# Two adapter products in one accumulation: all high-part products of a unit ahead of all low-part products

## The reference

```
w   = L0_cond_weight[itok]               # one 1024 x 1024 matrix for each of 8 samples
y   = einsum('bsi,boi->bso', x, w)       # x: 8 x 256 x 1024
t   = y.reshape(2048, 1024)[:, perm].reshape(2048, 16, 64)
t   = gelu(einsum('bhd,hdm->bhm', t, up))     # up: 16 x 64 x 256
t   = einsum('bhm,hmd->bhd', t, down)         # down: 16 x 256 x 64
out = x + t.reshape(2048, 1024)[:, unperm]
```

## Time and profile before

| | before |
|---|---|
| median of three runs | 297.74 us (297.6 to 298.1) |
| span of the profiled execution | 296.1 us |
| median of the runs less that span | 1.6 us |
| TensorE matmul busy (PE) | 290.6 us, 98% |
| TensorE weight load busy (PEld) | 215.0 us, 73% |
| VectorE (DVE) | 179.2 us, 61% |
| ScalarE (ACT) | 159.9 us, 54% |
| GpSimd (POOL) | 98.8 us, 33% |

### The profile page before, as it was taken

The page is one execution under the profiler, slowest core; times in us unless marked ns, Lnnn a source line. Parts: engine busy times, 40 slices in busy tenths (PEclk is TensorE's granted clock), DMA queues, the critical chain, the costliest instruction groups (busy, mean ns, idle before and its releaser), DMA issues.

```text
span 296.1 us, 4358 instructions
## 1 busy us (share of the span) xinstructions
PE 290.6 (98%) x1694; PEld 215.0 (73%) x1694; DVE 179.2 (61%) x211; ACT 159.9 (54%) x179; POOL 98.8 (33%) x92
## 2 busy tenths in 40 slices
PE   8999999999999999999999999999999999999994
PEld 7788888888888838886488855888468885444441
DVE  3599679589778455973658726685446523343333
ACT  5655453466764368344584265822853207777750
POOL 4000000068552007860527007702473405222234
PEclk9999999999999999999999999999999999999999
DMA  7999999999988947799576973876752864421335
GB/s 206 363 402 421 395 421 422 366 320 375 394 328 277 378 153 197 281 360 406 212 249 196 345 311 114 312 237 199 244 191 83 286 185 122 128 71 71 144 142 212
DMA packets 23699, 77.87 MB, mean 263 GB/s; under 512 B 2688, under 2 KB 11264, under 8 KB 18816
## 3 DMA queue, kind: packets, MB, share of 16 engines
q1 hardware_dynamic: 7056, 43.39, 39.3%
q0 software_dynamic: 7488, 25.18, 24.7%
q10 hardware_dynamic: 9136, 9.05, 8.8%
HBM read 60.82 MB, written 16.78 MB: 262 GB/s over the span
## 4 chain that ended last, share of the span: by engine, by line
PE 95%; DMA 2%; SPq 1%; POOL 1%; issue 0%; DVE 0%; ACT 0%; POOLq 0%; DVEq 0%
PE ps L641 38%; PE ps L645 19%; PE ps L698 19%; PE ps L674 6%; PE ps L677 5%; PE ps L680 5%; PE ps L606 2%; DMA w_raw<-w 2%; PE ps L611 1%; POOL out_late L319 1%; SPq L223 1%; SPq L251 0%; DVE w_raw L528 0%; ACT w_hi L429 0%; POOLq L361 0%
## 5 line engine op out<-in xcount | busy, mean ns | idle before, releaser
L641 PE MATMUL ps<-x_pair,w_hi 128*128 128x512 f32 x480 | 131.5, 395 | 0.0
L381 ACT ACTIVATE w_hi<-w_raw 128x1024 fp32r<-128x1024 f32 x58 | 58.3, 1056 | 62.8 <-PE ps L645 51.6
L415 ACT ACTIVATE hidden<-ps 128x1024 f32<-128x1024 f32 x64 | 61.6, 1028 | 55.1 <-PE ps L680 47.1
L641 PEld LDWEIGHTS ps<-x_pair,w_hi 128*128 128x128 f32 x480 | 82.0, 189 | 12.8 <-issue 1.8
L645 PEld LDWEIGHTS ps<-x_pair,w_lo 128*128 128x128 f32 x480 | 73.6, 189 | 10.2
L490 DVE TENSOR_TENSOR w_lo<-w_raw,w_hi 128x1024 fp32r<-128x1024 f32 x60 | 71.0, 1222 | 11.8 <-ACT w_hi L381 10.7
L645 PE MATMUL ps<-x_pair,w_lo 128*128 128x256 f32 x480 | 76.3, 281 | 0.0
L292 POOL DMA_INDIRECT t_raw<-y_rows,idx x32 | 34.9, 1090 | 115.1 <-DMA y_rows<-y_out 82.4
L518 DVE TENSOR_REDUCE y_out<-ps 128x256 f32<-128x512 f32 x64 | 42.8, 685 | 24.5 <-PE ps L645 23.0
L698 PE MATMUL ps<-hidden,down_sb 128*64 128x512 f32 (+1 forms) x264 | 57.4, 583 | 0.0
L510 DVE TENSOR_TENSOR t_lo<-t_raw,t_hi 128x512 fp32r<-128x512 f32 x32 | 21.7, 694 | 47.9 <-ACT t_hi L405 42.5
(11 more groups left out here) (29 smaller groups left out, 119.4 us busy)
## 6 DMA issues: line engine op xcount, KB each, us to landing
w_raw<-w SPq DMA_DIRECT2D x29, 1024.0 KB
y_rows<-y_out ACTq DMA_DIRECT2D x32, 256.0 KB
x_raw<-x_cols SPq DMA_DIRECT2D x7, 1024.0 KB
w_raw<-w SPq DMA_DIRECT2D x4, 256.0 KB, 5.0
w_raw<-w SPq DMA_DIRECT2D x2, 512.0 KB, 7.7
hidden<-up SPq DMA_DIRECT2D x1, 1024.0 KB, 12.3
down_sb<-down SPq DMA_DIRECT2D x1, 1024.0 KB, 12.3
w_raw<-w SPq DMA_DIRECT2D x2, 384.0 KB, 6.9
```

The source lines that it names most:

```text
L381: nc.scalar.activation(w_hi[:, g % WS, k, :], w_raw[:, g % WRAW, k, :], ACT.Copy).then_inc(w_hi_done, 1)
L415: nc.scalar.activation(hidden[:, f % HS, m, :, :], up_banks(f, m)[:, :, :], ACT.Gelu).then_inc(gelu_done, 1)
L641: nc.tensor.matmul(acc, w_hi[:, ws, k, col], x_pair[:, xs, k, :, :], start=(k == 0), stop=False)
```

## The change

In `lora_unit`, all sixteen products with w_hi (both output tiles, eight blocks each) now come first, and all sixteen with w_lo after them. The number and the shapes of the products, their operands, and what each waits for are the same; what is changed is which product carries each wait, and when each output tile is finished. `lora_done` for o = 0 is now raised by the eighth low product of the unit, and for o = 1 by the last product, as before.

```diff
                 for o in range(OT):
                     col = slice(o * P, (o + 1) * P)
-                    acc = y_bank(g, o)
-                    for n in range(2):
-                        ks = range(n * HALF, (n + 1) * HALF)
-
-                        if o == 0:
-                            pe.wait_ge(w_hi_done, 2 * (g - PAIR) + n + 1)
-                        for k in ks:
-                            nc.tensor.matmul(acc, w_hi[:, ws, k, col], x_pair[:, xs, k, :, :], start=(k == 0), stop=False)
-                        if o == 0:
-                            pe.wait_ge(w_lo_done, 2 * (g - PAIR) + n + 1)
-                        for k in ks:
-                            last = nc.tensor.matmul(acc[:, 0, :], w_lo[:, ws, k, col], x_hi[:, xs, k, :], start=False, stop=(k == KT - 1))
+                    for k in range(KT):
+                        if o == 0 and k % HALF == 0:
+                            pe.wait_ge(w_hi_done, 2 * (g - PAIR) + k // HALF + 1)
+                        nc.tensor.matmul(y_bank(g, o), w_hi[:, ws, k, col], x_pair[:, xs, k, :, :], start=(k == 0), stop=False)
+                for o in range(OT):
+                    col = slice(o * P, (o + 1) * P)
+                    for k in range(KT):
+                        if o == 0 and k % HALF == 0:
+                            pe.wait_ge(w_lo_done, 2 * (g - PAIR) + k // HALF + 1)
+                        last = nc.tensor.matmul(y_bank(g, o)[:, 0, :], w_lo[:, ws, k, col], x_hi[:, xs, k, :], start=False, stop=(k == KT - 1))
                     last.then_inc(lora_done, 1)
```

## The result

| | before | after |
|---|---|---|
| median of seven runs each | 297.9 us (297.56 to 298.95) | 296.4 us (295.85 to 297.15) |
| ratio, 95% interval | | 0.9947 [0.9933, 0.9962] |
| span of the profiled execution | 296.1 us | 295.2 us |
| TensorE matmul busy | 290.6 us | 289.7 us |

The change makes the kernel 0.5% faster, 1.5 us between the medians. I had forecast 297.5 with a range from 296.6 to 299.1 and "no measurable change": wrong, on the fast side. Rival B, the cost of a switch that is paid less often, is the one that came in kind.

The account below looks back on a forecast made before the run. TensorE's row of products was taken as the bound, with no wait to remove. Runs of sixteen gave -0.3 us, all else 0, on a 296.1 us span plus 1.6 around it: 297.4, given as 297.5, range 296.6 to 299.1.

Parts of the forecast that it names:

- Rival B: Switches between high and low products cost 0.01 us and three of four go: -0.9 us, 296.8 us; chance 0.17.
- part 4: TensorE's reads of w_lo: first half wanted 3.7 us into the unit, not 0.93; no wait removed, gain 0.
- part 3: TensorE's reads of w_hi: second half wanted 0.93 us into the unit, not 1.40; still in time, cost 0.
- Part 5: Output tile 0 finished 4.65 us into the unit, not 2.8; VectorE's second sum stays where it is, cost 0.
- part 2: Runs of sixteen for runs of four: high run 3.69 us, low 1.91, unit 5.60 against 5.61; -0.3 us over thirty.
- The lower end: Low bound for runs of sixteen, fitted from 4 + 4 and 6 + 6 lengths: unit 5.585 us, -0.9 us in all.
- A: Within each unit's sixteen high and sixteen low products, long runs go slower: up to +1.8 us, 299.5 us; chance 0.14.
- C: In all units, long runs reach `down_unit`'s 0.219 us per high product: -10.5 us, 287.2 us; chance 0.03.
- E: A TensorE wait on w_lo is removed after all: a few tenths of a us at most, counted inside the forecast.

Follow-up runs that it names:

- e8: Changed kernel with odd units reordered: two high products (k = 0), all 16 low, then the other 14 high; 296.57 us, ratio 0.9958 to the kernel before.

## Why the prediction was wrong

**Right.** That TensorE's spacings are the whole matter and no wait is removed (part 4; the moved-back waits confirm it). That w_hi, wanted earlier, is in time (part 3). Part 5, by which VectorE's first sum stands about 4.87 us behind a unit's start: in unit 15, which starts at 94.50, the sums stand at

```profile
99.37 0.69 DVE L518 TENSOR_REDUCE y_out<-ps 128x256 f32<-128x512 f32 x1 [1.16 <-PE ps L643]
100.26 0.69 DVE L518 TENSOR_REDUCE y_out<-ps 128x256 f32<-128x512 f32 x1 [0.20 <-PE ps L643]
```

that is 4.87 us behind the start. Ahead of the second 0.20 are idle, where part 5 left 0.28; the second sum stayed at the end of its unit. The low run, forecast at 1.91 us, took 30.08 - 28.17 = 1.91.

**The step that failed** is the value taken in part 2, the high run of 3.69 us; it took 3.65. I carried on the pace of the third to sixth high product of the run of six, 0.230, as if it were settled. It was the tail of a transient: 0.2325 in the mean of the first four, and 0.2267 in the mean from the fifth on. The error is 0.04 us a unit, about 1.1 us in all, the whole difference between the 297.5 forecast and the 296.4 measured. The unit of 5.567 us is below 5.59, which the prediction had named as a sign of being wrong.

**The lower end was too near as well.** The fit 4p + c and 6p + c gave c = 9 ns and -0.9 us. It takes the cost of a return as the same in both runs. With the settled p of 0.3467 the 4 + 4 group has 1.403 - 1.387 = 0.016 and the 6 + 6 piece 2.10 - 2.08 = 0.02: the longer run had paid the whole transient, the shorter one not yet. A fit over two lengths of which neither is settled put part of the transient into the slope. That I set the better fit aside for its thin digits, and then took a number from rows just as thin, made it worse.

**The rivals.** A (long runs at 0.235) is refuted: the 0.235 is the start of a transient, and wide products hold 0.2267. B was right in kind, a cost at the switch; its size was 1.2 us over the thirty units, not 0.9. C did not come: the settled 0.2267 and 0.120 stay above the 0.219 and 0.1095 that C would have brought. They are also about 11 ns each above the estimates of 216 and 109 ns that the prediction worked out from the Trainium skill ("TensorE: Matmul & The Clock Gate", "Wait — 56ns, not 53.3ns?"). E is refuted.

**What the runs make of it.** Excess over the settled unit of 5.547 us:

| run length | returns to high in a unit | unit, us | excess, ns |
|---|---|---|---|
| 1 | 16 | 5.653 | 106 |
| 2 | 8 | 5.576 | 29 |
| 4 (before) | 4 | 5.613 | 66 |
| 8 | 2 | 5.587 | 40 |
| 16 (changed) | 1 | 5.567 | 20 |
| 2 and 30 high, 16 low (e8) | 1 (every second one for two products only) | 5.555 | 8 |
| any, one width | 0 | | 0 |

From four on, with low products of 256 columns, each return to the wide products costs 16 to 20 ns, and the gain follows from the number of returns: this is shown. For runs of two and one that rule fails, and why two is cheap is open. The spacings of the trace say only where. In nanoseconds, a unit of the changed kernel has high products of 233, 236, 228, 233 and 231, then eleven of 227, and low ones of 113 and 119, then fourteen of 120. The loss builds up over the first four or five wide products, and the first narrow ones behind them give part of it back, so a return cut off after two wide products hardly pays. What in the array or its queue makes that transient no run here tells.

## What to carry to other kernels

Where TensorE's products are what bounds a kernel, order products by their width: put those of one width in a row, and count the returns from narrow to wide. Here that held for runs of four and more; runs of two did nearly as well, so measure the orders. Before carrying a pace from a short run to a longer one, look whether it is still falling along the run, and if it is, give the range the room for it. Where the effect is a few ns per product, read it from the spacing over many units in the trace, since the start-up of this kernel alone scatters by more than the gain.

## What was not expected of the hardware

- A product of 128 x 512 fp32r values settles at 0.2267 us start to start, but takes 0.2325 in the mean for the first four behind narrower products. Behind an `up_unit` stage it is slow for longer: unit 12 of the changed kernel is 0.13 us above unit 13 (5.69 against 5.567).
- In groups of four, widths 512 and 384 in turn cost 60 to 80 ns a unit, 512 and 256 cost 66, 512 and 512 none.
- Behind sixteen products of 128 columns, sixteen of 512 took 3.74 us, against 3.66 behind products of 256.
- With 128 columns a product still took 0.112 us. An estimate from it: under some 240 columns ((0.112 / 0.120) x 256) a product of this kind gains nothing more; no run has a width between 128 and 256.
- Alternating one by one was the dearest order of all (106 ns a unit), alternating two by two among the cheapest (29).
